# Values' products of the first attention: one block of two steps in every fourth unit in place of a block of one step in every second unit

## The reference, cut to what matters

```python
q, k = rope(rms_norm(q)), rope(rms_norm(k))
attn = einsum('bhqd,bhkd->bhqk', q, k) * scale
attn = softmax(where(causal, -inf, attn))
out = einsum('bhqk,bhkd->bhqd', attn, v)
x = x + out.reshape(Bc, Tc, C) @ w_proj.T
```

## Time and profile before

| | |
|---|---|
| median of 3 executions | 1649.47 us (1647.91 to 1651.11) |
| the profiled execution, its own time | 1651.36 us |
| its span in the trace | 1649.5 us |
| TensorE busy | 1539.1 us (93%) |
| VectorE busy | 1279.5 us (78%) |
| ScalarE busy | 941.4 us (57%) |
| V (L772) in the first attention | 1280 matmuls, first at 83.4 us, last at 600.3 us |
| mean granted clock of TensorE | 0.984 |

### The profile page before, as it was taken

The page is one execution under the profiler, slowest core; times in us unless marked ns, Lnnn a source line. Parts: engine busy times, 40 slices in busy tenths (PEclk is TensorE's granted clock), DMA queues, the critical chain, the costliest instruction groups (busy, mean ns, idle before and its releaser), DMA issues.

```text
span 1649.5 us, 27712 instructions
## 1 busy us (share of the span) xinstructions
PE 1539.1 (93%) x8432; PEld 995.5 (60%) x8432; DVE 1279.5 (78%) x2597; ACT 941.4 (57%) x1582; POOL 831.8 (50%) x922
## 2 busy tenths in 40 slices
PE   5799999999999987779999999999999999999998
PEld 3555565565565556557667566566566565666565
DVE  7798788688688537778788888878888888887765
ACT  3446756756765652345656655655655656556653
POOL 4350000000001123568668879788789699698553
PEclk9799999999999999889999999999999999999999
DMA  2000000000000000000000000000000000000000
GB/s 64 1 1 1 1 1 1 1 1 1 1 1 1 1 14 13 1 1 13 1 13 1 1 13 1 1 13 1 13 1 1 13 1 1 1 1 1 1 7 20
DMA packets 13673, 9.40 MB, mean 6 GB/s; under 512 B 3744, under 2 KB 13536, under 8 KB 13536
## 3 DMA queue, kind: packets, MB, share of 16 engines
q1 hardware_dynamic: 13536, 7.63, 1.6%
HBM read 6.58 MB, written 1.05 MB: 5 GB/s over the span
## 4 chain that ended last, share of the span: by engine, by line
PE 59%; POOL 17%; DVE 14%; issue 5%; ACT 4%; DMA 0%; DVEq 0%; SPq 0%; ACTq 0%; POOLq 0%
PE ps L954 9%; PE ps L738 8%; PE ps L772 7%; PE ps L757 7%; PE ps L921 5%; PE ps L942 4%; POOL gs L1694 4%; PE ps L943 4%; PE ps L694 4%; POOL gsum L1695 3%; POOL z L596 3%; POOL onm L590 3%; POOL h_qk L1696 2%; DVE gt L1518 2%; DVE mxp L1350 2%
## 5 line engine op out<-in xcount | busy, mean ns | idle before, releaser
L1209 ACT ACTIVATE pbuf<-ps 128x512 f32<-128x512 f32 x512 | 301.7, 600 | 166.5 <-PE ps L943 162.9
L1064 ACT ACTIVATE pbuf<-ps 128x1024 f32<-128x1024 f32 (+3 forms) x320 | 280.2, 897 | 185.2 <-PE ps L760 93.0
L1350 DVE TENSOR_REDUCE mxp<-ps 128x1 f32<-128x512 f32 (+2 forms) x432 | 278.9, 685 | 74.0 <-PE ps L738 52.2
L1566 DVE TENSOR_TENSOR den<-den,pbuf 128x1024 f32<-128x1024 f32 x224 | 310.6, 1387 | 1.9
L954 PE MATMUL ps<-pbuf,h_v 128*64 128x512 f32 x1024 | 247.9, 605 | 0.0
L1518 DVE TENSOR_TENSOR gt<-ps,gate 128x320 f32<-128x320 f32 x384 | 181.4, 483 | 77.6 <-POOL h_v L1704 48.0
L738 PE MATMUL ps<-kM,qT 128*128 128x512 f32 (+3 forms) x640 | 229.4, 410 | 10.2 <-ACT kM L1051 6.7
L1195 ACT ACTIVATE relu<-ps 128x512 f32<-128x512 f32 x256 | 152.2, 598 | 147.8 <-PE ps L921 111.4
L1539 DVE CUSTOM_DVE_ANT_0 relu<-ps,relu 128x512 f32<-128x512 f32 x256 | 174.2, 684 | 66.1 <-PE ps L921 60.2
L942 PE MATMUL ps<-q1T,k1T 128*128 128x512 f32 x512 | 214.5, 419 | 10.7 <-ACT pbuf L1209 9.1
L943 PE MATMUL ps<-q2T,k2T 65*128 65x512 f32 x512 | 203.3, 397 | 0.0
(11 more groups left out here) (235 smaller groups left out, 2714.9 us busy)
## 6 DMA issues: line engine op xcount, KB each, us to landing
wraw<-in_Wkv SPq DMA_DIRECT2D x16, 160.0 KB, 2.6
wraw<-in_Wq SPq DMA_DIRECT2D x8, 160.0 KB, 2.2
x<-in_x SPq DMA_DIRECT2D x4, 256.0 KB, 3.8
out<-x SPq DMA_DIRECT2D x4, 256.0 KB, 2.4
wqkv<-in_wqkvT SPq DMA_DIRECT2D x1, 192.0 KB, 3.7
masks<-in_masks SPq DMA_DIRECT2D x1, 128.0 KB, 4.9
dft<-in_dft SPq DMA_DIRECT2D x1, 128.0 KB, 2.3
wout<-in_Wo SPq DMA_DIRECT2D x2, 64.0 KB, 2.2
```

The lines of the kernel that those rows point to most:

```text
L1064: nc.scalar.activation(pbuf0[:, u % NP0, :, off:CH], ps[:, b:b + 2, off:CH], ACT.Exp, scale=float(D0) ** -0.5).then_inc(s_exp, 1)
L1209: nc.scalar.activation(pbuf1[:, u % NP1, i, :], ps[:, i, :], ACT.Exp, scale=float(D1) ** -0.5).then_inc(s_exp1, 1)
L1350: v.tensor_reduce(mxp[:, i, h:h + n, b], sc.rearrange("p (h k) -> p h k", h=n), AX.X, ALU.max).then_inc(s_read0d, 1)
L1566: v.tensor_tensor(dn, dn, w, ALU.add).then_inc(s_den1, 1)
```

## The change

`foreground0` gives V in other units. Before, in every even unit `u` it gave V of step `u/2 - 2`, directly behind S of that unit (and what preparation had its place in between). Now it gives two V's, of steps `k - 1` and `k = (u - 3)/2`, in every unit with `u % 4 == 1`. Steps 0 and 1 come in unit 5 (before: in units 4 and 6), steps 2 and 3 in unit 9 (before: 8 and 10), and so on: the first of each pair one unit later than before, the second one unit earlier. O goes with the last V of its chunk and so comes one unit earlier; F stays where it was.

```diff
@@ -423,9 +423,9 @@
             if half == 0:
                 return [("S", u)] if u < 2 * N0 * NG else []
             seq = []
-            k = u // 2 - 2
-            if u % 2 == 0 and 0 <= k < N0 * NG:
-                seq.append(("V", k))
+            k = (u - 3) // 2
+            if u % 4 == 1 and 0 <= k < N0 * NG:
+                seq += [("V", k - 1), ("V", k)]
                 if k % N0 + 1 in LAST0:
                     seq.append(("O", k // N0, LAST0.index(k % N0 + 1)))
             k = u // 2 - 4
```

## The result

The changed kernel takes 1656.9 us in the median of 7 executions (1655.94 to 1658.81); beside it the kernel before takes 1651.11 (7 executions). The ratio is 1.0039, with a 95% interval of 1.0027 to 1.0051: slower by 6 us, where 5.5 us less were forecast. The predicted range ended at 1656.0.

The account below looks back on a forecast made before the run. TensorE, busy 93% of the span, was taken as the bound, with VectorE and ScalarE limiting the ends. Terms -10.9 + 3.5 + 2, say -5.5 us, took 1651.36 to 1645.9 us (1644.0 against the median); range 1632.0 to 1656.0.

Parts of the forecast that it names:

- The saving of a pair: Each two-step V block in the first attention saves 0.33 us of TensorE time against two single blocks, before any waits.
- The middle: 54 stretches of 5 to 8 tiles between V blocks: 12 with no gain, 42 gaining 0.26 us; -10.9 us.
- The bare stretch: Eight tiles with four units of scores and nothing else: 6.1 us before and after, nothing gained.
- each further thing between the tiles: Masks, transposes or masked tiles give VectorE time, so bank waits go; 0.26 of 0.33 us saved in 42 stretches.
- The first group: 9 stretches of 10 to 12 tiles wait for banks VectorE still reads: 0.4 us each in the mean, +3.5 us.
- The end: Last group's end, 10 stretches without tiles: scores wait for exponentials, +0.7 us where bare, +2 us in all.
- Between the groups: 6 stretches with 0 to 3 tiles, paced by ScalarE's key copies: 0, with 3 us either way.
- Starved readers: Slower through three banks of maxima and two pairs of scores: 1663 us, or 1656 with half of it; chance 0.20.
- point of decision: With 8 tiles between blocks, a stretch passes its former 6.1 us when a tile takes 0.64 us.
- a drop of the clock inside the attention: Sign of a wrong forecast: the clock drops to 1.2 GHz inside the attention where TensorE now waits.
- the last V: Sign of a right forecast: the attention's last V stands at about 595 us.
- the second and third group's parts: Sign of a right forecast: these two parts of the attention become 3 to 4 us shorter each.

Follow-up runs that it names:

- short maxima: VectorE's row maxima of the first attention read only 128 columns of each tile: on the changed kernel 1623.94 us, on the kernel before 1633.12 us.
- short exponentials: From unit 288 on exponentials cover half their columns; units 287 to 319 take 42.63 us on the changed kernel, 42.30 on the kernel before.
- the other phase: Against the kernel before: pairs in units 4n + 3 except where a chunk ends between them, the rest single; 1651.73 us against 1650.17, ratio 1.0001.

## Why the prediction was wrong

**The saving of a pair: right.** 0.33 us by three edges. A pair with no wait behind it gave 0.31 to 0.34.

**The middle, -10.9 us: this step failed.** It is +2.9 in the changed kernel. The bare stretch was worked out rightly: 6.16 us from block to block for 6.1, and nothing gained. The failure is the sentence that each further thing between the tiles gives VectorE time and the waits go, and the 0.26 us for 42 stretches that hangs on it. In its place eight stretches lose 6.4 us and the other 46 gain 0.08 each. Three things were wrong in it, of which the first is the weakest. First, a diagonal unit was taken for more work on TensorE because it has mask matmuls. By the rows before, which stand below, a score matmul of 256 columns with its mask takes 0.17 us (340.09 to 340.26), less than the 0.235 of a full one. With 384 columns it is 0.23 (336.94 to 337.17), and only with 512 more, 0.29 (543.09 to 543.38). So masks don't ease a stretch in general. But that they made it worse isn't shown: among the 46, the 17 whose four units are all diagonal gain 0.13 us each, the other 29 0.05.

```profile
340.09 0.28 PE L757 MATMUL ps<-qT,kM 128*128 128x256 f32 x1
340.20 0.22 PE L760 MATMUL ps<-maskr,identr 128*128 128x128 f32 x1
340.26 0.33 PE L757 MATMUL ps<-qT,kM 128*128 128x256 f32 x1
```

Second, the weight load behind a wait lies open: a tile of 384 columns took 0.44 us where it had waited (320.19) and 0.34 where it hadn't (319.89), 0.10 more. I charged that where I found a wait by working through the bare stretch, and took 0 for all that I didn't work through. Third, other things wait for the same three banks: the transposes. The key copies at unit 53, first before, then changed:

```profile
178.17 0.63 PE L694 MATMUL ps<-ident,oT 128*128 128x128 f32 x4 [1.18 <-ACT kM L1051]
```

```profile
178.14 2.37 ACT L1051 ACTIVATE kM<-ps 32x512 fp32r<-32x512 f32 x4
...
180.66 0.63 PE L694 MATMUL ps<-ident,oT 128*128 128x128 f32 x4 [2.12 <-ACT kM L1051]
```

ScalarE's copies take as long as before, but the V that stood in this wait has gone into the pair ahead of it. TensorE comes 1 us earlier and waits 2.12 in place of 1.18. It costs 0.77 us at unit 53, and as much at 133, and short maxima leave 0.67 and 0.68 of it, so here it isn't VectorE. At unit 173, where queries are transposed, the same is a part; before:

```profile
364.85 1.07 PE L772 MATMUL ps<-pbuf,stagev 128*32 128x512 f32 x8
...
365.44 0.59 ACT L1055 ACTIVATE qT<-ps 128x512 fp32r<-128x512 f32 x1
...
366.88 0.60 PE L694 MATMUL ps<-ident,oT 128*128 128x128 f32 x4
```

and changed:

```profile
367.71 1.02 ACT L1064 ACTIVATE pbuf<-ps 128x1024 f32<-128x1024 f32 x1 [2.31 <-PE ps L757]
...
368.63 0.59 ACT L1055 ACTIVATE qT<-ps 128x512 fp32r<-128x512 f32 x1
...
369.36 0.63 PE L694 MATMUL ps<-ident,oT 128*128 128x128 f32 x4 [0.32 <-ACT qT L1055]
```

Before, the copy of the queries ran beside V. Now the pair stands ahead of it, and the next transposes come before the copy has freed their bank. That is 0.32 of the 0.86 us lost here. With short maxima the place loses nothing, so the larger part hangs on VectorE's reads. The run with short maxima is the evidence for the banks as a whole: there the middle gains 8.6 us, near the 10.9 that I had forecast with full ones. Why the pairs in units 273 and 277 lose 0.65 and 1.31, most of it with short maxima too, stays open.

**The first group, +3.5: right**, +2.56 in the change and +2.54 alone. VectorE's idle time behind a full pair is 1.45 us, where 0.33 stood behind a full single block; I had 0.9 to 1.3. With short maxima the loss turns into a gain of 1.7 us, so it is the banks, as the prediction had it.

```profile
123.89 8.14 DVE L1350 TENSOR_REDUCE mxp<-ps 128x1 f32<-128x512 f32 x13
133.48 3.68 DVE L1350 TENSOR_REDUCE mxp<-ps 128x2 f32<-128x512 f32 x6 [1.45 <-PE ps L742]
```

**The end, +2: right**, +2.28, and nearly gone with short exponentials. The bare stretch shows the times of the prediction to a few hundredths:

```profile
583.25 1.92 PE L772 MATMUL ps<-pbuf,stagev 128*32 128x512 f32 x16
...
585.11 1.20 PE L757 MATMUL ps<-qT,kM 128*128 128x512 f32 x4
585.88 3.79 ACT L1064 ACTIVATE pbuf<-ps 128x1024 f32<-128x1024 f32 x4 [1.50 <-PE ps L757]
586.96 0.30 PEld L757 LDWEIGHTS ps<-qT,kM 128*128 128x128 f32 x2 [1.08 <-ACT pbuf L1064]
586.96 0.73 PE L757 MATMUL ps<-qT,kM 128*128 128x512 f32 x2 [0.65 <-ACT pbuf L1064]
587.87 0.30 PEld L757 LDWEIGHTS ps<-qT,kM 128*128 128x128 f32 x2 [0.62 <-ACT pbuf L1064]
587.87 0.73 PE L757 MATMUL ps<-qT,kM 128*128 128x512 f32 x2 [0.18 <-ACT pbuf L1064]
588.53 1.93 PE L772 MATMUL ps<-pbuf,stagev 128*32 128x512 f32 x16
```

From block to block 5.28 us (forecast 5.3, before 4.6), the third unit's scores 1.85 behind the first's, the fourth's 2.76. ScalarE idles for 1.50 us, not 1.

**Between the groups, 0 within 3 us: -2.75.** Within the bounds by luck: no gain was foreseen. -0.72 at each of three places is the pair's own and the wait that it ends; some -0.67 more at each of units 125 and 205 is recovery of what the middle had lost; unit 41 loses 0.56. So a part of the middle's failure stands here with the other sign: middle and between the groups together are +0.16, where -10.9 were forecast.

**The rivals.** Starved readers came true, by its place and with about half its price: 0.05 us lost per stretch of the middle in the mean, and that as 0.42 to 1.31 in eight of them, not 0.25 in thirty. Its point of decision, a tile of 0.64 us, was put on VectorE's pace alone; the rows had 0.61 to 0.63, and it came true all the same, through the open loads and the transposes. That a drop of the clock inside the attention would make the forecast wrong was on the list; the trace of the change shows none. Three of the experiments' traces do (pairs in the middle, short maxima with pairs, short exponentials with pairs), each for 3.4 us. Of the other signs, the last V was to start at about 595 us and starts at 604.5, and the second and third group's parts were to be 3 to 4 us shorter each and are 0.3 (units 83 to 163 and 163 to 243).

## What to carry to other kernels

Two blocks merged save their edges, and uncover what the second one had stood in front of: read at each place what waits behind it for a bank or a reader, and take the saving place by place. Where the order is a list, the lag at equal work, read from two traces, shows what each place gives, and most of it comes again to 0.03 us in another kernel. What doesn't is a gain behind a loss, which may be recovery. Pairs at 19 of the 80 places and at 16 of the other phase's made a kernel faster by 0.6% out of a change that cost 0.4%. A term that is worked out for one kind of stretch should not be carried over to the others by a word like "eased"; the one of them that looks safest is to be worked through as well.

## What the runs showed of the hardware

Blocks of four column tiles of 32, plain float32, follow each other from step to step without a gap: the four passes of the pair at 316.37 us start 0.45, 0.43 and 0.43 us apart, the middle distance being that from one step to the next, and the pair is 1.85 us where two single blocks are 2.00. The edges between 32 columns and full width cost 0.085 us in front, and 0.14 and 0.105 behind. A full-width tile that had waited took 0.10 us more than the same one that hadn't. TensorE's clock fell to 1.2 GHz for 3.4 us at 179 us in one run, behind 4 us in which it was busy for 1.88, and in another behind a wait of 2.13 us at the same place. The kernel before and the change had waits of 1.18 and 2.12 us there and kept 2.4 GHz.
